# Expert stages: the down products stand ahead of the next pair's gate and up products, except in the last steps

## The reference

```python
def _swiglu(x, wg, wu, wd):
    return jax.nn.silu(x @ wg) * (x @ wu) @ wd
shared = _swiglu(x, wg_s, wu_s, wd_s) * RATIO
affinity = jax.nn.sigmoid(jnp.einsum('bsh,eh->bse', x, centroids))
biased = affinity + gate_bias
_, top_idx = jax.lax.top_k(biased, K)
...
routed = jnp.zeros_like(x)
for e in range(E):
    routed = routed + mask[..., e:e + 1] * _swiglu(x, wg[e], wu[e], wd[e])
return shared + routed
...
x = x + 0.5 * _L1_ffn_ref(_layernorm(x, axis=-1), L1_ffn_centroids, ...)
```

## Time and profile before

| | us |
|---|---|
| median of 3 runs | 860.14 |
| lowest and highest | 857.88, 861.78 |
| the profiled execution's own time | 868.81 |
| its span | 867.6 |
| PE busy | 730.7 (84% of the span) |
| DVE, ACT, POOL busy | 603.1, 375.6, 361.8 |
| mean granted clock of PE | 0.909 of full speed |

### The profile page before, as it was taken

One profiled execution on the slowest core, in us unless ns is written; L12 is line 12 of the kernel. 1 busy time (PEld: TensorE's weight loads), 2 busy tenths in 40 slices (PEclk: granted clock), 3 DMA queues, 4 the chain that ended last, 5 costly groups with the idle time before them and its releaser, 6 DMA issues. The chain is left out here.

```text
span 867.6 us, 11766 instructions
## 1 busy us (share of the span) xinstructions
PE 730.7 (84%) x3803; PEld 480.5 (55%) x3803; DVE 603.1 (70%) x1060; ACT 375.6 (43%) x756; POOL 361.8 (42%) x436
## 2 busy tenths in 40 slices
PE   3978799789999898889948969987969979898990
PEld 2766555344433476568825645654536645466880
DVE  6987644666661387756438898888999999984333
ACT  4321233335556343413304765687646645331330
POOL 4344122212011332524631037774858868361562
PEclk9989667789887999989979989998999999998995
DMA  4946623013366150146540000000006000023535
GB/s 184 320 55 89 99 37 49 6 26 105 107 198 198 51 242 30 63 125 186 162 151 1 0 1 1 1 1 1 1 13 279 0 1 2 30 87 94 158 113 181
DMA packets 46637, 74.75 MB, mean 86 GB/s; under 512 B 8258, under 2 KB 36674, under 8 KB 45010
## 3 DMA queue, kind: packets, MB, share of 16 engines
q1 hardware_dynamic: 42066, 61.61, 25.4%
q0 software_dynamic: 4512, 12.39, 4.0%
HBM read 35.45 MB, written 30.47 MB: 76 GB/s over the span
## 5 line engine op out<-in xcount | busy, mean ns | idle before, releaser
L1319 PE MATMUL PS<-FB,C 128*128 128x512 f32 x256 | 129.4, 610 | 3.5 <-DVE FB L2017 3.5
L1424 ACT ACTIVATE FA<-PS 128x512 f32<-128x512 f32 (+3 forms) x192 | 80.7, 496 | 71.2 <-PE PS L1065 70.7
L2124 POOL DMA_INDIRECT GY<-FB x62 | 61.1, 986 | 76.0 <-DVE FB L1905 47.5
L2096 POOL TENSOR_SCALAR_AFFINE_SELECT FA<-FA 128x128 f32<-128x128 f32 x128 | 36.3, 295 | 130.7 <-ACT FA L1424 128.5
L1715 DVE TENSOR_REDUCE FA<-PS 128x2 f32<-128x1024 f32 (+2 forms) x64 | 67.8, 1086 | 18.1 <-PE PS L1044 17.8
L2148 POOL TENSOR_TENSOR FB<-FB,RBF 128x512 f32<-128x512 f32 x51 | 66.0, 1295 | 30.0 <-DVE FB L2008 29.9
L929 PE MATMUL PS<-TRI 128*128 128x512 bf16 x201 | 54.1, 414 | 14.3 <-DMA FB<-GY 12.0
L1065 PE MATMUL PS<-RA 64*128 64x512 f32 (+3 forms) x192 | 60.0, 501 | 5.0 <-ACT FA L1424 5.0
L1200 PE MATMUL PS<-WE,FB 128*128 x248 | 63.6, 402 | 0.6 <-ACT FB L1463 0.6
L1319 PEld LDWEIGHTS PS<-FB,C 128*128 128x128 f32 x256 | 46.9, 197 | 28.3 <-issue 20.1
L1065 PEld LDWEIGHTS PS<-RA 64*128 64x128 f32 x192 | 29.3, 223 | 52.3 <-ACT FA L1424 31.0
(11 more groups left out here) (282 smaller groups left out, 1646.5 us busy)
## 6 DMA issues: line engine op xcount, KB each, us to landing
GX<-ZT SPq DMA_DIRECT2D x4, 4160.0 KB, 15.0
WE<-in_wr SPq DMA_DIRECT2D x8, 1536.0 KB, 10.8
FB<-GX SPq DMA_DIRECT2D x62, 130.0 KB, 2.2
RA<-RA SPq DMA_DIRECT2D x48, 128.0 KB, 4.8
FB<-GY SPq DMA_DIRECT2D x8, 512.0 KB, 5.6
FA<-in_w SPq DMA_DIRECT2D x2, 1024.0 KB, 7.1
FA<-in_qkvo SPq DMA_DIRECT2D x1, 1536.0 KB, 19.6
FB<-in_we SPq DMA_DIRECT2D x4, 384.0 KB, 3.6
```

Source lines behind the costliest of these rows:

```text
L1319: pe.matmul(bank(m), ident, shc[k % 4], start=n == 0, stop=n == DN - 1).then_inc(*yad.inc(ch, n, m))
L1424: act.activation(PT[n % 12][:, c0:], bank(ring_bank[(x, *a)])[:, c0:], ACT.Exp, scale=0.25).then_inc(*exd.inc(*a))
L2124: pool.indirect_dma_start(GY, bass.IndirectOffsetOnAxis(ap=ids[:, b:b + 1], axis=0), yout[pi % 4][:, (b - b0) * D:(b - b0) * D + D], None) ...
```

## The change

In the loop of `moe_steps`, e4 and back of pair i−3 move ahead of e2 of pair i−1 as long as i < n. In the last three rounds they stand behind e2 as before, but ahead of e3 where before they stood behind it.

```diff
-        if 0 <= i - 1 < n:
-            yield [("e2", u, i - 1)]
+        opened = [("e2", u, i - 1)] if 0 <= i - 1 < n else []
+        down = [("e4", u, i - 3), ("back", u, i - 3)] if 0 <= i - 3 < n else []
+        yield down + opened if i < n else opened + down
         if 0 <= i - 2 < n:
             yield [("e3", u, i - 2)]
-        if 0 <= i - 3 < n:
-            yield [("e4", u, i - 3), ("back", u, i - 3)]
         if i < n and i % 2 == 0:
```

## The result

| | before | changed |
|---|---|---|
| median of 4 runs, us | 860.96 | 893.22 |
| lowest and highest | 857.88, 867.11 | 891.49, 900.06 |
| the profiled execution's own time | 868.81 | 893.29 |

The changed kernel takes 1.039 times as long (interval 1.034 to 1.044), about 32 us more. The forecast was +24.5 us and its range ended at 891: the direction was right, the size a quarter too small.

The account below looks back on a forecast made before the run. PE was taken to bound the expert loops, rounds growing from 3.25 to 4.18 us by the wait for DVE's copy and register reads. 10.3 + 10.9 + 2 × 1.65 = +24.5 us on 860.14 gave 884.6, range 878 to 891.

Parts of the forecast that it names:

- The loop of PE, ACT, DVE and PE again: In each expert round, PE waits for DVE's copy, standing still 0.85 us before the down product.
- POOL's pause ahead of pair 13's first write: At each expert loop's end, POOL was to stand idle about 1.6 us before that write.
- the prediction's own signs of being wrong: In the expert loop: rounds staying at 3.25 us, rounds exceeding 4.5 us, or a clock under 1.00.
- the size of the round: In both expert loops, a round was to go from 3.25 to 4.18 us, 0.93 more.
- The register reads: On PE, reads queue behind the down product's wait; 0.03 and 0.05 us of them show per round.
- The prediction's bound of 0.2 a read: If an unprefetched PE register read takes 0.2 us more, 24 × 0.2 adds 5 us: 889.4.
- the split of pair 3: DVE weight split in the first block, late for its load in the trace; taken as costing nothing.
- The last rounds: From pair 12's down product to the last write, 11.75 us against 10.1: +1.65 for each block.
- The first down products: At each loop's start: 395.0 against 395.50 in the first block, 801.4 (1.1 us earlier) in the second.
- The faster one: Rival: no hole opens, writes start 2.8 us earlier in both loops, −5.6 us, 854.5; chance 0.04.
- The clock: Rival: holes halve PE's clock in half of the 24 rounds, +31 us, 915; chance 0.08.
- The third: Rival: PE products run closer behind holes, up to 0.42 us back per round, 874.5; chance 0.05.

Follow-up runs that it names:

- e5: Changed kernel with a second, unused DVE copy ahead of the real one that the down product needs; 894.32 us in one run.
- e6: Kernel before with the same second, unused DVE copy ahead of the real one; 856.29 us in one run.
- e1: New order in the first mixture block only, the second keeping the order of before; 883.59 us, 1.014 of before.
- e2: Changed kernel with PE's reads of the expert numbers moved one round ahead of their use; 890.64 us, 1.024 of before.
- e3: Changed kernel with DVE making the copy for the down product ahead of its product of the next pair; 882.81 us, 1.013 of before.
- e8: Order of before in all rounds except the last three, which have the changed order; 860.02 us, 1.002 of before.
- e7: Changed kernel with DVE copying out all down products, where ACT copied out those of odd pairs; 890.36 us in one run.
- e11: Kernel before with its steps rotated so the loop is one round shorter, and register reads a round earlier; 862.32 us, 1.003 of before.
- e14: Changed kernel with all Mamba weight loads and splits of the first block moved behind its loop; 887.38 us in one run.

## Why the prediction was right in direction and short in size

**Right.** The loop of PE, ACT, DVE and PE again decides. The copy ready 1.38 us after e3, the down product 1.51 (1.5 predicted), PE busy 84% of the second loop (84), the clock 1.00 there, L1895 as the releaser. That the copy is on the path now and was not before is shown by e5 and e6, and that nearly all of the price lies in the rounds by e1, e2, e3 and e8. POOL's pause ahead of pair 13's first write was 1.8 us over the usual 0.30 (1.6 predicted). One of the prediction's own signs of being wrong came: rounds over 4.5 us, in the first block on the average (4.53) and in the second in some rounds (up to 4.67).

**Short, step by step.** Measured 32.6 us against 24.5. The step that failed is the size of the round: 4.18 us predicted, 4.41 measured in the second block, and 5.89 for the first round of the first. The mechanism stands; these terms of the sum were too small. The range, up to 891, had room for the reads and the spread of the runs alone.

1. *The first pass behind a hole.* The prediction took 0.87 us for a down product, from a queue that was full. Behind a hole it is 0.96: the first pass takes 0.316 to the next start, the others 0.216. The weight loads, in the round shown above and in that of the earlier trace rows:

```profile
815.48 0.73 PEld L1219 LDWEIGHTS PS<-WE,FB 128*128 128x128 f32 x4 [0.93 <-issue]
...
812.12 0.73 PEld L1220 LDWEIGHTS PS<-WE,FB 128*128 128x128 f32 x4
```

   Behind the hole load and product both start at 815.48; before, the load at 812.12 stood 0.11 ahead of its product at 812.23, beside the pass ahead. That the open weight load is the 0.1 is a reading of these rows; no run varies it. The Trainium skill ("TensorE: Matmul & The Clock Gate", on LDWEIGHTS) says that PE loads weights ahead of products in flight, and that a load takes the number of columns over 1.2 in ns. By that page an unhidden load of 128 columns is an estimated 107 ns; the trace has 100. Cost: 24 × 0.1 = 2.4 us.
2. *The register reads.* Predicted 0.08 a round, measured 0.20 (changed against e2), for 24 rounds 2.9 us more. The prediction's bound of 0.2 a read was the right place to look, but somewhat over half of it is what came. Most of it is reads that take up to 0.68 us instead of 0.30. The Trainium skill ("DMA: Bandwidth & Descriptors", among the measured latencies) gives about 600 ns as the least that a `tensor_load` takes; the rows with 0.297 contradict it as a floor here, and the measurement decides.
3. *The first block's split.* The prediction looked at the split of pair 3 and took nothing for it; that one was indeed covered. The one it passed over stands ahead of the first copy. It named the danger ("should one be late once, it costs about 1 us") but not the place, and not that the hole would be long enough for the clock to fall behind it: first round 5.89 instead of 4.27, so 1.6 us in this execution (and in e5's), none in those of e1 and e7.
4. *The ends.* The last rounds were taken at +1.65; they came at 11.98 − 10.1 = +1.87 in both blocks. The step was right; the round in it was 4.4 and not 4.18. The first down products came 0.34 and 0.33 us later than predicted (9.50 and 8.11 us after the first gate product), the first behind the late split, the second because the second pair's gate and up took 2.34 us and not 2.00.

Together 2.4 + 2.9 + 1.6 + 0.4 + 0.7 = 8.0 of the 8.1 us missing.

**The rivals.** The faster one is out: the hole opened in every round. The clock fell in none of the second block's rounds, and in the first round of the first block. The third, that PE makes part up because its weight loads fill only 27.96 of 32 us, is not only out but the wrong way round: nothing ran closer than 0.216 us behind a hole, and the first pass ran wider. In this kernel the even distance of starts, not the share of the weight loads, told how full PE was.

**Open.** Why some reads are long. And whether the kernel before can be beaten by this kind of change: the nearest, e11, can't be told from it.

## What to carry to other kernels

Before a product is put nearer to what makes its input, add up the answer of the other engines (here 1.38 us over ACT and DVE, and 0.13 until PE starts) and the work that would stand in between (0.65): in this kernel the difference was paid in every round, one to one. To it come the things that a full queue had hidden, the register reads and addresses in the stream, and 0.1 us of the first product behind each hole; a trace of the full queue shows them at their hidden price only. And look at the first round by itself, since a side job that waits for a transfer hurts once the work it delays is next in line.

## What was not expected of the hardware

- The first 256-column pass behind a hole: 0.316 us to the next start instead of 0.216, at full clock, for holes of 0.17 to 3.08 us alike.
- A register read on PE took 0.30 us in most cases and up to 0.71 in some, in a stream that ran ahead (0.54 in the first block of before) as in one that had waited (0.68). With no packet in flight beside its start none took over 0.32; cause open.
- Holes of 0.69 us in every 4.4 us left the granted clock at 1.00 for the whole loop. Holes of 3.08 to 3.54 us were followed by products at part or half clock; behind those of 1.51 to 1.82 us ahead of a first down product none was seen.
- Two of POOL's indirect writes took 1.22 and 2.20 us instead of 0.96 while DVE split 128x1536 beside them (e14). The other traces agree: of 928 writes with no split beside their first 0.96 us none took over 0.97, of 64 with one 27 took over 1.0.
